# One transformer block: second norm and MLP inside the next batch's attention, one ring for all weight tiles, engine loops written out

## The chip, the cores and the metric

One core of a Trainium2 chip runs the kernel. The metric is the device time of one launch in microseconds. Three runs of the kernel before gave 3036.27, 3036.28 and 3037.81; the median is 3036.28.

## The reference

Four sequences of 512 tokens go through one block: an embedding lookup, attention with grouped heads, and a block-diagonal MLP on permuted features.

```python
h = tok(x)                     # sum of 8 shard lookups with clipped index, + 8 * bias + position
h = h + attn(layernorm(h))     # 32 heads in 8 groups of 4, head size 128, causal softmax, one k and v per group
h = h + ffn(layernorm(h))

def ffn(x, up, down, perm):    # 16 blocks of 64 features, 256 hidden each
    t = x.reshape(b * l, Dm)[:, perm].reshape(b * l, h, d)
    t = gelu(einsum('bhd,hdm->bhm', t, up), approximate=False)
    t = einsum('bhm,hmd->bhd', t, down)
    return t.reshape(b * l, h * d)[:, unperm].reshape(b, l, Dm)
```

Everything is float32, with 4 batches, 512 tokens and 1024 features.

## The kernel before

Every float32 factor is split into a rounded high part (float32r, a copy on ScalarE) and a low part (the rest: a subtraction on VectorE, or on GpSimd for weights), and each product is three matmuls (L403 to L405: high by high, low by high, high by low). Activations are held with features on the partitions, 8 blocks of 128 x 512.

The work is a list of named steps, and every engine walks the same list in order, doing its own part of each step. Nothing is reordered at run time: an engine that waits in one step holds up its part of all later ones. The steps:

- `S0`..`S3`: scores of a head of the group (L424), row maxima (VectorE, L827), exponentials (ScalarE, L655). `N0`..`N3`: scaling of its rows by the inverse sum (VectorE, four operations, L837).
- `Ta`, `Tb`: transposes of the probabilities (L436), rounded by ScalarE (L661 to L667), low part by VectorE (L842 to L851). `PV`: probabilities by values (L457), rounded at L670, low part at L855.
- `Q0`..`Q3`, `K`, `V`: projections, 24 matmuls each (L476). Q0, Q1, K and V of a unit belong to the next group; Q2 and Q3 to the present one. `VT` transposes V.
- `D0`..`D7`: a tile of the dense layer of the group before, 12 matmuls (L487), added to the residual `hacc` by VectorE (L871).
- `H`: the residual is transposed in from the gathered token rows (L517). `G`, `A`, `B`, `La`, `Lb`, `X`: gather of the token rows by GpSimd, addition of positions (GpSimd, L1043) and of the shard edges (a small product, L534, added by VectorE), layer norm per token, and transposes into the normalised input `xn`.

A unit is one group of one batch. A batch is `FIRST`, six turns of `MID` in a loop, `LAST`, and `POST`; the four batches are a loop of three and a copy (L321 to L323). `POST` has the last group's dense tiles, the sums for the second norm (`M`, `R`: matmuls by a matrix of ones, L567), the projections for the next batch, and then `I` and `F`: the MLP, alone, in 8 pairs of blocks (L573). Of a pair, four products `up` (3 matmuls each) go into the two banks of `fb`, ScalarE applies gelu (L754), VectorE rounds (a cast, L963) and takes the low part (L966; of the first of four, GpSimd, L1074), and four products `down` add up in one bank. The input of a pair is gathered from a scratch copy in DRAM (GpSimd, L1051), centred and scaled by VectorE, rounded by ScalarE, low part by VectorE (L946). The output rows are scattered by GpSimd (L1065).

Jobs (projections, dense tiles, `up` products, `H`) alternate between the two banks of `fb`; a job waits for the semaphore of the bank that the job two before it used (L470). Edge products use `sc`, the input transposes `tp`, the MLP outputs `pv` and `sc`.

Weights come by SP's DMA queue into raw buffers: two of 128 x 1024 for the projections with three slots of high and low parts (`RQ`), two of 128 x 512 for the dense layer with four slots (`RD`), and two slots each for the MLP's. ScalarE rounds a tile in the step of the job that frees its slot, GpSimd takes the low part (L996, L1001), and SP loads the next tile once GpSimd is done with a raw buffer. The last of MID's order is `S3 PV1 K N3 Q1 Ta3 PV2 Tb3 V PV3 VT`.

Of the kernel before, what the change touches and what calls it, by code (L numbers as in the profile page):

```python
# [39 lines left out]


# [14 lines left out]
POST = ("D0 X0 X1 M0 D1 X2 X3 M1 D2 X4 X5 M2 D3 X6 X7 M3 D4 M4 D5 M5 D6 M6 D7 M7 Q0 R0 R1 K R2 R3 Q1 R4 R5 R6 R7 "
        "I V VT F").split()
POST_PE = ("D0 X0 X1 D1 M0 X2 X3 D2 M1 X4 X5 D3 M2 X6 X7 D4 M3 D5 M4 D6 M5 D7 M6 Q0 M7 K R0 R1 Q1 R2 R3 R4 R5 R6 R7 "
           "V VT F").split()
START = "G A0 B0 B1 A1 B2 B3 A2 B4 B5 A3 B6 B7 La Lb X0 X1 X2 X3 X4 X5 X6 X7 Q0 K Q1 V VT".split()


def is_job(s):

    return s[0] in "QKDH" or s == "V"  # L80


def number(steps, which):

    out, n = {}, 0
    for s in steps:
        if which(s):
            out[s] = n
            n += 1
# [3 lines left out]
def is_qkv(s):

    return s[0] in "QK" or s == "V"


def is_split_job(s):

    return s[0] in "QK"  # L100


class Place:

    def __init__(self, steps, b, g, kind):
        self.b, self.g, self.steps, self.kind = b, g, steps, kind
        self.n = 8 * b + g
        if kind == "start":  # L110
            self.half, self.split, self.wq = 0, 0, 0
        elif kind == "post":
            self.half, self.split, self.wq = 56 + 76 * b, 3 + 40 * b + 37, 4 + 48 * b + 44
        else:
            self.half, self.split, self.wq = 2 + 76 * b + 7 * g, 3 + 40 * b + 5 * g, 4 + 48 * b + 6 * g
        self.wd = 64 * b + 56 if kind == "post" else 64 * b + 8 * (g - 1)

        self.wq_tile = 0 if kind in ("start", "post") else 4 + 6 * g
        self.wd_tile = 56 if kind == "post" else 8 * (g - 1)
        self.jobs = number(steps, is_job)  # L120
        self.splits = number(steps, is_split_job)
        self.weights = number(steps, is_qkv)

    def bank(self, s):
        return self.jobs[s] % 2

    def full(self, s):

        return 2 * self.half + (self.jobs[s] + 1)

    def free(self, s):

        return self.half + self.jobs[s] // 2

    def split_done(self, s):
        return self.split + (self.splits[s] + 1)

    def wq_at(self, s):

        return self.wq + self.weights[s]  # L140

    def wq_slot(self, s, n, ahead=0):
        first = {"start": 0, "post": 48}.get(self.kind, 4)
        return (first + self.weights[s] + ahead) % n
# [1004 lines left out]
```

## Time and profile before

| what | us |
|---|---|
| median of three runs | 3036.28 |
| span of the profiled execution | 3036.1 |
| first scores, from the start | 92.3 |
| one unit of MID | 75.75 |
| MLP of a batch, alone | 80.6 |
| busy: TensorE, VectorE, ScalarE, GpSimd | 2774.6, 1627.7, 1243.6, 1047.4 |

PE is TensorE, PEld its weight loads, DVE VectorE, ACT ScalarE, POOL GpSimd, SP SyncE. PEclk is the granted share of TensorE's clock: 1.00 is 2.4 GHz, 0.50 is 1.2 GHz. Matmuls are pipelined, so the duration of one is longer than its pace; the pace is read from start to start.

### The profile page before, as it was taken

The page shows a single profiled execution, that of the slowest core. Times are in us where ns is not written, and L with a number is a line of the kernel's source. Part 1 is how long each engine was busy: PE and PEld are TensorE (multiplying, and loading weights), DVE is VectorE, ACT ScalarE, POOL GpSimd, SP SyncE. Part 2 cuts the span into 40 slices and gives each one's busy share as a digit, 9 for nine tenths or more (in the row PEclk, how much of TensorE's full clock was granted, in tenths as well). Part 3 has the DMA queues.
Part 4 walks back from the last instruction along what each step waited for, and adds up shares of the span by engine and source line. Part 5 has one row for each costly group of instructions (what it writes and reads, how often), then busy time and mean ns, then how long its engine had stood idle before and what let it go on. Part 6 is the DMA issues. An engine that isn't in the chain of part 4 may idle for free.

```text
span 3036.1 us, 42337 instructions
## 1 busy us (share of the span) xinstructions
PE 2774.6 (91%) x13344; PEld 2291.2 (75%) x13344; DVE 1627.7 (54%) x3524; ACT 1243.6 (41%) x2791; POOL 1047.4 (34%) x647
## 2 busy tenths in 40 slices
PE   2899999988789999998879999999877999999966
PEld 1788888876578888886657888888756888888844
DVE  4444444455844444446675444444586444444558
ACT  2434444435344444444434444444344444444343
POOL 3433333323443333332435333333153333333224
PEclk9999999999899999999989999999988999999978
DMA  3322222213232222221323222222232222222121
GB/s 103 102 93 69 69 69 69 69 46 108 91 112 70 69 69 69 69 69 46 104 74 118 70 69 69 69 69 69 64 96 77 70 69 69 69 69 69 45 87 63
DMA packets 88977, 229.31 MB, mean 76 GB/s; under 512 B 10781, under 2 KB 10781, under 8 KB 88778
## 3 DMA queue, kind: packets, MB, share of 16 engines
q1 hardware_dynamic: 81450, 202.87, 21.0%
q0 software_dynamic: 7424, 25.17, 2.5%
q8 instruction: 52, 0.85, 0.1%
q14 instruction: 51, 0.42, 0.0%
HBM read 211.22 MB, written 16.78 MB: 75 GB/s over the span
## 4 chain that ended last, share of the span: by engine, by line
PE 81%; DVE 9%; issue 5%; ACT 4%; POOL 1%; DMA 1%; DVEq 0%; SPq 0%; ACTq 0%; POOLq 0%
PE fb L403 19%; PE fb L404 19%; PE fb L405 19%; PE tp L436 4%; DVE g_hi L963 3%; PE sc L403 3%; PE pv L403 3%; PE sc L404 3%; PE sc L405 3%; PE pv L404 3%; PE pv L405 3%; PE sc L567 1%; DVE h_tok L887 1%; DVE y_lo L946 1%; ACT row_buf L638 0%
## 5 line engine op out<-in xcount | busy, mean ns | idle before, releaser
L996 POOL TENSOR_TENSOR wq_lo<-wq_raw,wq_hi 128x1024 fp32r<-128x1024 f32 x193 | 462.6, 2397 | 1238.2 <-ACT wq_hi L617 1234.0
L403 PE MATMUL fb<-xn_hi,wq_hi 128*128 128x512 f32 x1536 | 609.3, 397 | 13.5 <-ACT hacc L695 12.1
L404 PE MATMUL fb<-xn_lo,wq_hi 128*128 128x512 f32 x1536 | 604.6, 394 | 0.0
L405 PE MATMUL fb<-xn_hi,wq_lo 128*128 128x512 f32 x1536 | 604.0, 393 | 0.0
L1001 POOL TENSOR_TENSOR wd_lo<-wd_raw,wd_hi 128x512 fp32r<-128x512 f32 x256 | 331.6, 1296 | 511.4 <-ACT wd_hi L627 494.0
L403 PE MATMUL fb<-at_hi,wd_hi 128*128 128x512 f32 x1024 | 411.9, 402 | 6.2 <-DVE at_lo L855 6.2
L655 ACT ACTIVATE prob<-sc,neg_max 128x128 f32<-128x128 f32 (+3 forms) x512 | 263.3, 526 | 370.7 <-DVE neg_max L830 370.7
L404 PE MATMUL fb<-at_lo,wd_hi 128*128 128x512 f32 x1024 | 404.7, 395 | 0.0
L405 PE MATMUL fb<-at_hi,wd_lo 128*128 128x512 f32 x1024 | 404.5, 395 | 0.0
L403 PEld LDWEIGHTS fb<-xn_hi,wq_hi 128*128 128x128 f32 x1536 | 292.6, 190 | 75.3 <-ACT hacc L695 9.7
L871 DVE TENSOR_TENSOR hacc<-hacc,fb 128x512 f32<-128x512 f32 x256 | 175.7, 686 | 313.5 <-PE fb L405 312.6
L405 PEld LDWEIGHTS fb<-xn_hi,wq_lo 128*128 128x128 f32 x1536 | 291.7, 190 | 61.8
L404 PEld LDWEIGHTS fb<-xn_lo,wq_hi 128*128 128x128 f32 x1536 | 292.2, 190 | 60.1
L627 ACT ACTIVATE wd_hi<-wd_raw 128x512 fp32r<-128x512 f32 x240 | 152.0, 633 | 370.4 <-PE fb L405 351.4
L855 DVE TENSOR_TENSOR at_lo<-pv,at_hi 128x512 fp32r<-128x512 f32 x128 | 88.6, 692 | 348.9 <-ACT at_hi L670 348.3
L837 DVE TENSOR_SCALAR prob<-prob,inv_sum 128x128 f32<-128x128 f32 (+3 forms) x512 | 258.1, 566 | 4.5
L827 DVE CUSTOM_DVE_ANT_0 sc<-sc,mask 128x128 f32<-128x128 f32 (+3 forms) x512 | 236.3, 521 | 15.5 <-PE sc L405 14.8
L677 ACT ACTIVATE q_hi<-fb 128x512 fp32r<-128x512 f32 x128 | 76.6, 599 | 399.8 <-PE fb L405 399.8
L403 PEld LDWEIGHTS fb<-at_hi,wd_hi 128*128 128x128 f32 x1024 | 192.4, 188 | 50.3 <-issue 5.3
L405 PEld LDWEIGHTS fb<-at_hi,wd_lo 128*128 128x128 f32 x1024 | 192.3, 188 | 46.6
L404 PEld LDWEIGHTS fb<-at_lo,wd_hi 128*128 128x128 f32 x1024 | 192.6, 188 | 42.8
L859 DVE TENSOR_TENSOR q_lo<-fb,q_hi 128x512 fp32r<-128x512 f32 x128 | 88.5, 691 | 242.6 <-ACT q_hi L677 242.6
(140 smaller groups left out, 4796.3 us busy)
## 6 DMA issues: line engine op xcount, KB each, us to landing
wq_raw<-in_w_qkv SPq DMA_DIRECT2D x193, 512.0 KB, 3.5
wd_raw<-in_w_dense SPq DMA_DIRECT2D x256, 256.0 KB, 2.6
row_buf<-in_pos SPq DMA_DIRECT2D x16, 512.0 KB, 3.4
h_rows<-hacc SPq DMA_DIRECT2D x32, 256.0 KB, 2.0
up_raw<-in_w_up SPq DMA_DIRECT2D x32, 256.0 KB, 2.6
dn_raw<-in_w_down SPq DMA_DIRECT2D x32, 256.0 KB, 2.8
hacc<-in_x_row SPq DMA_DIRECT2D x3, 256.0 KB, 3.8
hacc<-h_rows,perm POOLq DMA_INDIRECT x32, 3.8
```

Of the source, the lines that this page charges most:

```text
L403: pe.matmul(dst, a_hi, b_hi, start=first, stop=False)
L404: pe.matmul(dst, a_hi, b_lo, start=False, stop=False)
L405: return pe.matmul(dst, a_lo, b_hi, start=False, stop=last)
L436: return pe.transpose(tp[:, bank, c:c + P], prob[:, P_OFF[t] + j * P:P_OFF[t] + (j + 1) * P], ident[:, :])
L627: act.activation(wd_hi[:, m % RD, :], wd_raw[:, m % 2, :], copy).then_inc(wd_rounded, 1)
L655: act.activation(prob[:, P_OFF[t]:P_OFF[t] + w], sc[:, bank, c:c + w], ACT.Exp, bias=neg_max[:, t:t + 1], scale=SCALE, accum_out=row_sum[: ...
L827: dve.tensor_tensor_reduce(at, at, mask[:, S - w:S], 1.0, LOWEST, ALU.add, ALU.max, row_max[:, t:t + 1]).then_inc(tile_max, 1)
L837: dve.tensor_scalar(at, at, inv_sum[:, t:t + 1], None, ALU.mult).then_inc(prob_ready, 1)
L871: dve.tensor_tensor(hacc[:, i, :], hacc[:, i, :], fb[:, place.bank(s), :], ALU.add)\
L963: dve.tensor_copy(g_hi[:, w // 2, w % 2, :], gelu_out(w)).then_inc(g_rounded, 1)
L996: pool.tensor_tensor(wq_lo[:, slot, :], wq_raw[:, raw, :], wq_hi[:, slot, :], ALU.subtract)\
L1001: pool.tensor_tensor(wd_lo[:, m % RD, :], wd_raw[:, m % 2, :], wd_hi[:, m % RD, :], ALU.subtract)\
```

## The change

The loops are gone: the program makes one list of all steps of all batches, and every engine's code is written out from it. The second norm and the MLP of batch b run in units 0 to 5 of batch b+1; only those of the last batch stay behind the last unit (`REST` and what follows it). New step letters: `Z` (transposes of the residual, statistics per token by VectorE), `Y` (mean and inverse deviation spread over the partitions by a product with ones, now float32), `F` (gather of a pair's input), `P` (that input centred by GpSimd, scaled by VectorE, rounded by ScalarE, low part by VectorE), `U` (an `up` product with gelu and, now, the rounding copy on ScalarE; low parts of even ones on GpSimd, of odd ones on VectorE), `O` (a pair's `down` products, 12 matmuls, added by VectorE to the gathered input, and scattered). In the lists small letters `f p u o` are the unit's first pair and `F P U` its second, whose `O` is the next unit's `q`. `Z`, `Y`, `B`, `X`, `U` and `O` are jobs in the two banks of `fb` like the others.

All weight tiles are 128 x 512, in one ring: 4 raw slots (`RAW`), 11 slots of high and low parts (`RW`). A projection takes two tiles. Tile m is rounded in the step of the user of tile m - 11, never before the step of an earlier tile; a pair's `up` tile has its last `U` as user. The positions are loaded straight into the token buffer, and the gather adds the rows to them (no `A` steps). Semaphores are per buffer.

```diff
+RAW, RW = 4, 11
-MID = ("S0 N0 Q2 D0 Ta0 D1 Tb0 S1 N1 Q3 D2 Ta1 D3 Tb1 S2 D4 D5 N2 D6 D7 PV0 "
-       "Ta2 Q0 Tb2 S3 PV1 K N3 Q1 Ta3 PV2 Tb3 V PV3 VT").split()
...
+FIRST = ("S0 N0 Q2 H0 H1 Ta0 H2 Tb0 S1 N1 Q3 H3 Ta1 H4 H5 Tb1 S2 H6 H7 N2 PV0 Q0 Ta2 Tb2 S3 PV1 K N3 Q1 Ta3 "
+         "PV2 Tb3 V PV3 VT")
+MID = ("S0 N0 Q2 D0 Ta0 D1 Tb0 S1 N1 Q3 D2 Ta1 D3 Tb1 S2 D4 D5 N2 D6 D7 PV0 Ta2 Q0 Tb2 S3 PV1 K N3 Q1 Ta3 "
+       "PV2 Tb3 V PV3 VT")
+STATS = ("S0 N0 Q2 D0 Ta0 D1 Tb0 S1 N1 Q3 D2 Ta1 D3 Tb1 S2 D4 D5 N2 D6 D7 Z0 PV0 Z1 Ta2 Z2 Q0 Z3 Tb2 S3 Z4 PV1 K "
+         "Z5 N3 Ta3 Q1 Z6 PV2 V Z7 Tb3 PV3 VT")
+MLP0 = ("S0 N0 Q2 Y0 H0 Ta0 Y1 H1 Tb0 f S1 H2 N1 Q3 H3 D0 p Ta1 H4 D1 Tb1 H5 S2 F D2 H6 N2 D3 H7 D4 D5 D6 D7 u0 PV0 u1 "
+        "Ta2 u2 Q0 u3 Tb2 S3 P PV1 o K N3 U0 Ta3 Q1 U1 PV2 V U2 Tb3 U3 PV3 VT")
+MLP = ("S0 N0 Q2 q D0 Ta0 f D1 Tb0 S1 N1 Q3 p D2 Ta1 D3 Tb1 S2 F D4 D5 N2 D6 D7 u0 PV0 u1 "
+       "Ta2 u2 Q0 u3 Tb2 S3 P PV1 o K N3 U0 Ta3 Q1 U1 PV2 V U2 Tb3 U3 PV3 VT")
+GATHER = ("S0 N0 Q2 q D0 G Ta0 D1 Tb0 S1 N1 Q3 D2 Ta1 D3 Tb1 S2 D4 D5 N2 D6 D7 PV0 Ta2 Q0 Tb2 S3 PV1 K N3 Q1 Ta3 "
+          "PV2 Tb3 V PV3 VT")
+EMBED = ("S0 N0 Q2 D0 B0 Ta0 D1 B1 Tb0 S1 N1 Q3 D2 B2 Ta1 D3 B3 Tb1 S2 D4 D5 N2 D6 D7 B4 PV0 B5 Ta2 Q0 B6 Tb2 S3 B7 "
+         "PV1 K N3 Q1 Ta3 PV2 Tb3 V PV3 VT")
+TURN = ("S0 N0 Q2 D0 Ta0 La D1 Tb0 S1 N1 Lb Q3 X0 Ta1 D2 X1 Tb1 S2 D3 D4 N2 X2 D5 X3 D6 X4 D7 X5 PV0 X6 Ta2 X7 Tb2 S3 "
+        "PV1 Q0 N3 K Ta3 Q1 PV2 Tb3 V PV3 VT")
+LAST = ("S0 N0 Q2 D0 Ta0 D1 Tb0 S1 N1 Q3 D2 Ta1 D3 Tb1 S2 D4 D5 N2 D6 D7 PV0 Ta2 Tb2 S3 PV1 N3 Ta3 PV2 Tb3 PV3")
+REST = "D0 D1 D2 D3 Z0 D4 Z1 D5 Z2 D6 Z3 D7 Z4 Z5 Z6 Z7 Y0 Y1"
...
+def schedule():
+    steps = unit(START, -1, 7)
+    for b in range(B):
+        steps += unit(STATS if b else FIRST, b, 0)
+        for g in range(1, 5):
+            steps += unit((MLP0 if g == 1 else MLP) if b else MID, b, g)
+        if b + 1 < B:
+            steps += unit(GATHER, b, 5) + unit(EMBED, b, 6) + unit(TURN, b, 7)
         else:
+            steps += [s for s in unit(GATHER, b, 5) if s.kind != "G"] + unit(MID, b, 6) + unit(LAST, b, 7)
+    steps += unit(REST, B, 0)
...
+        for m in range(RW, len(self.tiles)):
+            place = max(place, self.at[user[m - RW]])
+            self.splits[STEPS[place]].append(m)
...
+            def start_job(s):
+                if before(s) > 0:
+                    pe.wait_ge(bank_free[bank(s)], before(s))
+                return fb[:, bank(s), :]
...
+                elif s.kind == "P":
+                    n = PAIRS * s.b + s.i
+                    act.wait_ge(scaled, n + 1)
+                    if n > 0:
+                        act.wait_ge(job_full, full(Step("U", (n - 1) // PAIRS, 0, 4 * ((n - 1) % PAIRS) + 3)))
+                    act.activation(y_hi[:, :], y_raw[:, :], copy).then_inc(y_rounded, 1)
+                elif s.kind == "U":
+                    p, w = s.i // 4, s.i % 4
+                    n = 2 * (PAIRS * s.b + p)
+                    act.wait_ge(job_full, full(s))
+
+                    if n > 0 or w > 1:
+                        act.wait_ge(g_low_dve if w % 2 else g_low_pool, n + w // 2)
+                    act.activation(g_raw[:, w % 2, :], fb[:, bank(s), :], ACT.Gelu).then_inc(bank_free[bank(s)], 1)
+                    if p > 0 and w == 0:
+                        act.wait_ge(job_full, full(Step("O", s.b, 0, p - 1)))
+                    act.wait_ge(*free(s))
+                    act.activation(g_hi[:, w, :], g_raw[:, w % 2, :], copy).then_inc(g_rounded, 1)
+                for m in splits[s]:
+                    act.wait_ge(job_full, full(tally.user[m - RW]))
+                    split(m)
...
+                for m in splits[s]:
+                    if m + RAW < NT:
+                        sp.wait_ge(w_ready, m + 1)
+                        load(m + RAW)
```

On GpSimd, `low(m)` for the same tiles stands at the end of each step, behind the step's own gather, scatter, centring or low part. VectorE's part of a `Z` is one statistics operation; at `Z7` four aggregations, a reciprocal and eight scalings of the identity follow, with a square root on ScalarE between.

## Rows read from the trace of the kernel before

**Rows 1.** By stage: length; busy PE, PEld, DVE, ACT, POOL; PEclk, DMA share, GB/s.
```profile
0.00:92.29 92.29, 37.50 (x140) 27.16 (x141) 34.27 (x52) 21.08 (x26) 30.30 (x20) 1.00 0.31 100
...
236.64:312.39 75.75, 75.71 (x383) 64.06 (x382) 36.01 (x91) 30.88 (x75) 24.65 (x15) 1.00 0.22 69
...
752.40:832.96 80.56, 55.91 (x196) 40.15 (x194) 71.74 (x87) 33.00 (x58) 40.77 (x31) 0.87 0.26 83
2895.38:2948.34 52.96, 36.75 (x128) 24.75 (x129) 30.44 (x38) 21.35 (x34) 17.25 (x14) 0.78 0.38 114
2948.34:3036.10 87.76, 56.28 (x192) 41.85 (x192) 72.02 (x85) 30.21 (x54) 38.88 (x30) 0.81 0.19 60
```

**Rows 2.** Order of time, TensorE: start us, us, engine, line, operation; then idle before.
```profile
99.80 0.60 PE L523 MATMUL fb<-ident,h_tok 128*128 128x128 f32 x4
100.24 1.04 PE L436 MATMUL tp<-ident,prob 128*128 128x128 f32 x8
...
904.05 0.39 PE L403 MATMUL fb<-xn_hi,wq_hi 128*128 128x512 f32 x1
...
909.52 0.40 PE L403 MATMUL fb<-at_hi,wd_hi 128*128 128x512 f32 x1
...
912.32 1.03 PE L436 MATMUL tp<-ident,prob 128*128 128x128 f32 x8
```

**Rows 3.** Order of time, TensorE, two products of the MLP at full clock.
```profile
3002.13 0.39 PE L403 MATMUL fb<-y_hi,up_hi 128*128 128x512 f32 x1
...
3002.82 0.39 PE L403 MATMUL sc<-g_hi,dn_hi 128*128 128x512 f32 x1
```

**Rows 4.** Order of time, all engines, from K's end to head 3's turn in a plain unit.
```profile
295.88 0.39 PE L403 MATMUL fb<-xn_hi,wq_hi 128*128 128x512 f32 x1
...
296.08 0.60 ACT L677 ACTIVATE k_hi<-fb 128x512 fp32r<-128x512 f32 x1 [2.59 <-PE fb L405]
...
296.71 0.69 DVE L859 TENSOR_TENSOR k_lo<-fb,k_hi 128x512 fp32r<-128x512 f32 x1 [2.50 <-ACT k_hi L677]
...
297.52 3.45 DVE L837 TENSOR_SCALAR prob<-prob,inv_sum 128x128 f32<-128x128 f32 x4
...
297.71 2.39 POOL L996 TENSOR_TENSOR wq_lo<-wq_raw,wq_hi 128x1024 fp32r<-128x1024 f32 x1 [7.17 <-ACT wq_hi L617]
...
301.33 0.71 PE L436 MATMUL tp<-ident,prob 128*128 128x128 f32 x5
```

**Rows 5.** Order of time, VectorE: the four scalings with GpSimd idle.
```profile
840.26 1.28 DVE L837 TENSOR_SCALAR prob<-prob,inv_sum 128x128 f32<-128x128 f32 x4
```

**Rows 6.** Groups of instructions: busy us, mean ns of one, idle before.
```profile
L627 ACT ACTIVATE wd_hi<-wd_raw 128x512 fp32r<-128x512 f32 x240 | 152.0, 633 | 370.4 <-PE fb L405 351.4 <-DMA wd_raw<-in_w_dense 19.0
...
L1001 POOL TENSOR_TENSOR wd_lo<-wd_raw,wd_hi 128x512 fp32r<-128x512 f32 x256 | 331.6, 1296 | 511.4 <-ACT wd_hi L627 494.0 <-ACT wd_hi L673 17.1
```

**Rows 7.** Order of time: maxima, exponentials and what follows them, one head.
```profile
288.71 0.30 DVE L827 CUSTOM_DVE_ANT_0 sc<-sc,mask 128x128 f32<-128x128 f32 x1
...
290.85 0.37 ACT L655 ACTIVATE prob<-sc,neg_max 128x128 f32<-128x128 f32 x1 [2.53 <-DVE neg_max L830]
...
292.88 0.61 ACT L670 ACTIVATE at_hi<-pv 128x512 fp32r<-128x512 f32 x1
```

**Rows 8.** Busy time of the projection after a stop of 3.00 us.
```profile
120.73:129.00 8.27, 8.27 (x24) 6.56 (x25) 0.98 (x3) 0.96 (x2) 1.28 (x1) 0.65 0.36 129
```

**Rows 9.** Order of time in the last MLP: a VectorE cast beside two GpSimd operations.
```profile
3000.48 3.18 DVE L963 CAST g_hi<-g_raw 128x512 fp32r<-128x512 f32 x1 [0.56 <-ACT g_raw L754]
...
3000.82 1.30 POOL L1074 TENSOR_TENSOR g_lo<-g_raw,g_hi 128x512 fp32r<-128x512 f32 x1
...
3002.07 1.29 POOL L1006 TENSOR_TENSOR up_lo<-up_raw,up_hi 128x512 fp32r<-128x512 f32 x1
```

**Rows 10.** DMA issues of the page: size, median us from issue to landing.
```profile
wd_raw<-in_w_dense SPq DMA_DIRECT2D x256, 256.0 KB, 2.6
```

**Rows 11.** Order of time at the start: the last of four position additions.
```profile
44.25 2.34 POOL L1043 TENSOR_TENSOR h_tok<-h_tok,row_buf 128x1024 f32<-128x1024 f32 x1 [3.52 <-DMA row_buf<-in_pos]
```

More of the change, by code:

```diff
@@ L71 @@
[L71 to L89, printed above, removed]
-    return out
@@ L93, in is_qkv @@
[L93 to L113, printed above, removed]
-        else:
[L115 to L144, printed above, removed]
@@ new lines, with __init__ @@
+STEPS = schedule()
+JOBS = ("Q", "K", "V", "D", "H", "Z", "Y", "B", "X", "U", "O")
+class Tally:
+    def __init__(self):
+        jobs = [s for s in STEPS if s.kind in JOBS]
+        self.at = {s: n for n, s in enumerate(STEPS)}
+        self.job = {s: n for n, s in enumerate(jobs)}
+        self.qk = {s: n for n, s in enumerate(s for s in jobs if s.kind in ("Q", "K"))}
+        self.tiles, self.tile, user = [], {}, []
+        for s in jobs:
+            if s.kind in ("Q", "K", "V"):
+                which = {"Q": s.i, "K": HQ, "V": HQ + 1}[s.kind]
+                own = [("qkv", 2 * ((HQ + 2) * s.g + which) + half) for half in range(2)]
+            elif s.kind == "D":
+                own = [("dense", 8 * s.g + s.i)]
+            elif s.kind == "U" and s.i % 4 == 0:
+                own = [("up", s.i // 4)]
+            elif s.kind == "U":
+                self.tile[s] = self.tile[Step("U", s.b, 0, s.i - s.i % 4)]
+                user[self.tile[s]] = s
+                own = []
+            elif s.kind == "O":
+                own = [("down", s.i)]
+            else:
+                own = []
+            if own:
+                self.tile[s] = len(self.tiles)
+            self.tiles += own
+            user += [s] * len(own)
+        self.user, self.splits, place = user, {s: [] for s in STEPS}, 0
+        for m in range(RW, len(self.tiles)):
+            place = max(place, self.at[user[m - RW]])
+            self.splits[STEPS[place]].append(m)
@@ L147, in tower_kernel, with bank, full, before @@
 def tower_kernel(nc, x_cols, x_row, table, bias, pos, edge_cols, w_qkv, w_dense, w_up, w_down, perm_cols, out):
     scratch = nc.dram_tensor("h1_rows", [E, S], F32).ap()
+    weights = {"qkv": w_qkv, "dense": w_dense, "up": w_up, "down": w_down}
+    tally = Tally()
+    job, splits, tiles = tally.job, tally.splits, tally.tiles
+    NT = len(tiles)
+    def bank(s):
+        return job[s] % 2
+    def full(s):
+        return job[s] + 1
+    def before(s):
+        return job[s] // 2
+    def head(s):
+        return 4 * (8 * s.b + s.g) + s.i
```

1184 lines of the change are left out of this document (496 added, 688 removed).

## The prediction

> **What bounds the kernel now.** I read the busy times by stage first, then TensorE's order of time for the pace of each step, then one head's chain over all engines. An attention unit in the middle takes 75.75 us and TensorE works in 75.71 of them; VectorE is busy 36, ScalarE 31, GpSimd 25 [rows 1]. That unit is pure TensorE work at the full clock. The MLP is not: 80.56 us with TensorE busy 55.91 at a mean clock of 0.87, VectorE busy 71.74 [rows 1]. Start and end are latency too: 92.29 us before the first scores, and 52.96 + 87.76 us from the last unit's dense products on [rows 1]. So time can be won in three places: start, tail, and what the MLP and second norm take beyond their TensorE work. The other engines have room in the sum; the question is whether each engine's fixed order leaves room at each step, for all engines walk one list of steps.
>
> **Prices.** Start to start at full clock [rows 2]: projection 909.52 - 904.05 = 5.47 us, dense tile 912.32 - 909.52 = 2.80, four transposes 100.24 - 99.80 = 0.44. An MLP product of three matmuls is 3002.82 - 3002.13 = 0.69 [rows 3]; a pair needs four up (2.75) and four down (2.75), 5.5 us, eight pairs 43.8.
>
> **The work** if TensorE never waited, from the first scores to the last unit's end. Eight units are 606.0 us a batch. Batch 0: less 8 dense tiles (22.4), plus token and input transposes (8 x 0.44 each, 7.0) and eight edge products (1.9): 592.5. Batches 1 and 2: 606 + 7.0 + 1.9, plus 8 statistics transposes 3.5, two row broadcasts (1.0, as four transposes each; four times that at most), 43.8 of MLP: 663.2 each. Batch 3: less four projections (21.9), plus 3.5 + 3.5 + 1.0 + 43.8: 635.9. Sum 2554.8.
>
> **Waits that the new lists make.** I follow each engine through the MLP unit. The plain unit leaves little slack: K's product ends at 295.88, ScalarE rounds it at 296.08 for 0.60, VectorE takes the low part at 296.71, then come the four scalings of head 3, 3.45 us from 297.52 to 300.97, and TensorE turns that head at 301.33, because Q1's 5.47 us stand between [rows 4].
> (a) Head 3's turn. The MLP lists say K N3 U0 Ta3 Q1: only 0.69 us of TensorE work stands between K and the turn, while the scalings end 5.09 after K. TensorE waits 4.4. Undisturbed, the scalings take 1.28 [rows 5] and the wait is 2.2; that is the low end. I take 4.4, since GpSimd's two low parts after K (2 x 1.30 [rows 6], in place of the single one of 2.39 [rows 4]) start before the scalings. The statistics list (K Z5 N3 Ta3) has the same: Z5 covers 0.44, wait 4.7.
> (b) The input pair. "Q3 p D2 Ta1 D3 Tb1": GpSimd must first do Q3's two low parts, so centring ends about 5.3 after Q3 (0.7 + 2 x 0.63 of ScalarE, overlapped by GpSimd, then three operations of 1.30 [rows 6]). Scaling 0.69, rounding 0.63, low part 0.69 follow; VectorE and ScalarE stand in P meanwhile, then D2 and the turn's own split (0.6 + 0.7) come. Tb1 can run 8.8 after Q3; TensorE has D2, Ta1, D3 = 6.4. Wait 2.4 (1 to 4).
> (c) PV3 stands after Tb3 with U3 between, not V. ScalarE has v_feat, U2's gelu and copy, and Tb3's copy behind V, some 2.5 us with 0.4 of VectorE, PV3 is asked for at 1.6: wait 1.4 (0.5 to 2.8). In the statistics list, Z7's moments, two diagonals and a root on ScalarE stand there: wait 4.3 (3 to 6).
> (d) The ring. A tile is rounded at the step of the user eleven tiles back, in order. An up tile counts as used at its last product, so U0's tile and the four of Q1 and V are all split at U3: five on ScalarE, with four raw slots. The fifth must wait for GpSimd's first low part (1.30) and a load of 2.6 [rows 10]; ScalarE stands until about 9.0 after V. Behind it are PV3's and VT's roundings, so VectorE reaches the next S0 at 11.0, not at 7.6. Maxima take 2.1 and exponentials 2.0 [rows 7], scalings 1.3, Q2's low part 0.7: 17.5 undisturbed, 20 with GpSimd's lock. With the output product behind Q2, D0 shares Q2's bank and is due at 15.6. Wait 3.8 (2 to 6), 12 times.
> (e) The clock. Where TensorE idled 3.00 us before 120.73, the next projection took 8.27 us at a mean granted clock of 0.65, instead of 5.47 [rows 8]: back at the lower level, 1.2 GHz, for part of it. After (a) and (d) I charge 2.0 and 1.6 (0 to 5 together).
> An MLP unit thus waits 3.8 + 2.4 + 4.4 + 1.4 + 3.6 = 15.6. The first of a batch, without the wait of (d) but with H0 behind Q2 (1.5): 12.6. Statistics unit: 0.5 + 4.7 + 4.3 + 3.5 of clock = 13.0. The gather unit has (d): 5.4. Embed and turn units 2.0 together. Per batch 1 and 2: 13.0 + 12.6 + 3 x 15.6 + 5.4 + 2.0 = 79.8. Batch 3: 13.0 + 12.6 + 46.8 + 5.4, and 7.9 for its last unit, which has no projections to cover head 3 (rounding, low parts and scalings of some 2 to 3 us at three places) = 85.7. Batch 0: 3.8 for three turns of its first unit with little between their halves, and 1.5. Sum 250.6.
>
> What decides (a) and (d) is that a single VectorE cast, begun at 3000.48, lasted 3.18 us, more than the four undisturbed scalings together, until two GpSimd operations that began at 3000.82 and 3002.07 had ended, the second at 3003.36 [rows 9].
> The Trainium skill (SBUF — State Buffer, "Who interferes with whom") says otherwise on the order: whichever operation issues first holds the shared ports for its whole instruction and the other blocks. By that rule the scalings would slip in between GpSimd's two low parts and end 1.1 us sooner; over 15 such places the sum would be 16 us lower. The row shows the later GpSimd operations winning, so the sum goes by the row.
>
> **Start.** Four position blocks cost 3.52 of waiting for the load and 2.34 of GpSimd each [rows 11]; they vanish, as the gather adds onto the loaded positions. VectorE's part (four operations of 0.69 a block) becomes the bound, 12.5 us instead of 23.4, but gathers now wait for all four position loads, so it begins later. I take 6.5 less (11 less to 3 more): first scores at 85.8. The eleven first weight tiles cost GpSimd 14.3 behind the gathers and are just covered; uncovered, some 5 us.
> **Tail.** Eight dense tiles 22.4, transposes 3.5, statistics lagging 2, moments and root 5, broadcasts 1.7, gather 5 (it waits for the second broadcast), first input 3.4: 43 against 52.96. The lone MLP has the same chain per pair: two products, the output product, two products, then P; ScalarE now makes gelu and copy (1.2 each): 88 against 87.76. Together 131.5.
> Moved steps that cost nothing: table loads (two to gelu and two back per MLP unit, run in ScalarE's idle time), two gathers and two scatters per unit on GpSimd (taken at 1.3 each like a low part, 5 of the 50 us in which it is idle), and the position loads on SP; if GpSimd's wait for those outlasts the four raw slots, 0 to 3 us a batch. Written-out code has no loop end, but is fetched once and straight on.
>
> **Sum.** 85.8 + 2554.8 + 250.6 + 131.5 = 3022.7, plus 0.2 outside the span: 3023. The profiled span is 3036.1 and the median 3036.28, so they are one number. That is 0.4% less; a measurement can tell about 0.2%, 6 us, from no change. What is hidden, 3 x (80.56 - 43.8) = 110 us of MLP beyond its products and what the norm between batches idled, is nearly given back in many small waits.
>
> **Rivals.**
> 1. The waits form only in part. With (a) at 2.2, (b) at 1.0, (c) at 0.5, (d) at 1.0 and no clock lost, an MLP unit waits 4.7 and all waits sum to some 100: 2872. For: the plain unit runs without a wait on a slack of 0.36 us, and busy times leave room everywhere. Against: (a) follows from the order alone, and (d) from five tiles for four slots. Chance 0.25.
> 2. Slower: ScalarE's stand at U3 lasts longer, because GpSimd, which holds low parts, gathers and scatters in one order, comes late to the first of the five. Place: the fifth split of each MLP unit. Price 6 us and 2 more of clock, 12 times: +96, 3119; it decides from (3042 - 3023) / 12 = 1.6 us per unit on. For: every low part, gather and scatter stands in one queue, in the order of the list. Against: GpSimd idles half of the unit. Chance 0.22.
> 3. The waits are as sized, but start and tail give nothing back (6.5 + 9.2): 3039, no change. Chance 0.08.
> My forecast is the waits as sized, each sum within a sixth: 2985 to 3060, chance 0.45. Of it 0.27 lies below 3030, 0.05 within 0.2% of before, 0.13 above. So faster 0.25 + 0.27 = 0.52, the same 0.08 + 0.05 = 0.13, slower 0.22 + 0.13 = 0.35.
> Range: 2880 to 3085. The low end takes in most of rival 1 (about 0.1 is left below it), the high end (d) at 6, (b) at 4 and the clock at 5, and the milder half of rival 2 (0.1 above it).
>
> **What would show it.** The first scores near 86; plain units of batch 0 still 75.75; MLP units 100 to 104 with about 12 us of TensorE idle, of which 4.4 before head 3's turn with VectorE's scalings as releaser, about 4 before D0 on Q2's low part, 2.4 before Tb1; ScalarE idle 2 to 3 us at the fifth split on a weight load; GpSimd idle half the unit; after the last PV3, 131. If MLP units come out near 90, (a) to (d) are wrong; above 108, rival 2.

## The result, and the profile after

The changed kernel takes 3093.34 us (median of 4 runs, 3092.01 to 3103.49) against 3036.28 before: a ratio of 1.0197, with a 95% interval of 1.0183 to 1.0210. It is slower by 1.8 to 2.1%. Forecast were 3023, and 3085 as the high end. The profiled execution spans 3090.4 us.

The page of the changed kernel, its busy times and its granted clock:

```profile
PE 2751.3 (89%) x13360; PEld 2293.1 (74%) x13360; DVE 1356.6 (44%) x3303; ACT 1354.8 (44%) x3073; POOL 1113.8 (36%) x886
...
PEclk9999999999999999999999999999999999999976
```

No engine but TensorE is over half busy, and the granted clock is 90% or more in all but the last two of the 40 slices. None of TensorE's waits in this trace is put to the issue of its instructions (26.1 us were before), so nothing here points at the written-out code. The time by stage shows where it lies (columns as in [rows 1]): start, a plain unit, a gather unit of batch 0, a statistics unit, an MLP unit, a gather unit of batch 1, the norm behind the last unit, and the last batch's own MLP.

```profile
0.00:87.17 87.17, 37.53 (x140) 27.21 (x141) 29.69 (x53) 25.06 (x38) 31.09 (x27) 1.00 0.46 123
226.51:301.82 75.31, 75.18 (x383) 64.03 (x382) 35.58 (x91) 31.52 (x81) 25.47 (x21) 1.00 0.24 71
452.44:537.39 84.95, 78.05 (x384) 65.88 (x382) 36.65 (x91) 31.41 (x81) 31.70 (x25) 0.94 0.40 112
697.45:789.48 92.03, 82.65 (x415) 70.47 (x414) 43.84 (x113) 33.56 (x83) 27.03 (x22) 0.95 0.28 86
1090.99:1189.39 98.40, 89.98 (x432) 74.93 (x430) 42.11 (x101) 49.19 (x107) 42.45 (x35) 0.97 0.26 75
1189.39:1279.02 89.63, 80.30 (x395) 67.45 (x393) 37.06 (x92) 34.08 (x85) 37.93 (x30) 0.96 0.44 121
2889.07:2931.61 42.54, 29.12 (x132) 21.87 (x133) 14.33 (x32) 9.12 (x14) 13.49 (x11) 0.95 0.34 111
2931.61:3090.40 158.79, 67.83 (x192) 46.43 (x192) 25.99 (x38) 45.92 (x77) 49.03 (x42) 0.71 0.08 25
```

Set beside the forecast's terms (batches end where the next one's first scores begin; batch 3 at the dense products behind its last unit):

| stretch | forecast | profile |
|---|---|---|
| start | 85.8 | 87.2 |
| batch 0 | 592.5 + 5.3 = 597.8 | 610.3 |
| batch 1 | 663.2 + 79.8 = 743.0 | 741.6 |
| batch 2 | 743.0 | 744.1 |
| batch 3 | 635.9 + 85.7 = 721.6 | 706.0 |
| norm behind the last unit | 43 | 42.5 |
| lone MLP | 88 | 158.8 |

Up to the last norm the sum agrees: its dense products begin at 2889.07, forecast at 2891.2. That it agrees so closely is luck, as batch 0 is 12.5 us over and batch 3 is 15.6 us under. The miss of the whole, 71 us, is in the last row. There TensorE is busy 67.8 us of 158.8; before, 56.28 of 87.76 [rows 1]. So 11.5 us of the 71 are the same 192 matmuls at a lower granted clock (0.71 against 0.81), and 59.5 are time in which TensorE stands. TensorE's waits in that stretch (us in all, times, longest):

```profile
PE fb L378 <- DVE y_lo L782: 71.7, 8, 10.3
PE fb L378 <- ACT g_raw L625: 8.4, 7, 1.2
PE fb L378 <- DVE hp L790: 7.4, 7, 1.1
```

The first of the eight stops, 7.68 us, stands ahead of the stretch's first product, as one of 7.72 did before. The next is 6.6 us, and the other six are 9.1 to 10.3 each: one stop a pair, for the input of the next pair. The order of time of one pair shows what stands behind it:

```profile
3004.54 0.80 PE L378 MATMUL fb<-y_hi,w_hi 128*128 128x512 f32 x1 [9.11 <-DVE y_lo L782]
...
3011.13 0.63 ACT L629 ACTIVATE g_hi<-g_raw 128x512 fp32r<-128x512 f32 x1 [4.30 <-PE fb L380]
...
3013.59 0.68 DVE L790 TENSOR_TENSOR hp<-hp,fb 128x512 f32<-128x512 f32 x1
...
3014.55 1.01 POOL L846 DMA_INDIRECT out_rows<-hp,perm_out  x1 [1.43 <-DVE hp L790]
...
3017.57 0.96 POOL L825 DMA_INDIRECT hp<-h_rows,perm  x1 [2.01 <-DMA out_rows<-hp,perm_out]
3018.55 1.27 POOL L840 TENSOR_TENSOR g_lo<-g_raw,g_hi 128x512 fp32r<-128x512 f32 x1
3021.11 1.26 POOL L836 TENSOR_TENSOR y_raw<-hp,mean 128x512 f32<-128x512 f32 x1 [1.29 <-DMA hp<-h_rows,perm]
...
3024.54 0.80 PE L378 MATMUL fb<-y_hi,w_hi 128*128 128x512 f32 x1 [9.26 <-DVE y_lo L782]
```

Two up products and pair p-1's down products run from 3004.54 to 3011.10. ScalarE may not write U0's copy until then (one set of rounded GELUs, all read by those twelve matmuls). The addition follows, the scatter, its landing, only then the gather of pair p+1 into the slot that the scatter has left, its landing, centring, scaling, rounding, low part: 20.00 us from one pair's first product to the next's. Before, all eight gathers went into the residual's eight blocks ahead of the lone MLP, so that no transfer stood in the loop; the input had two sets, the raw GELUs four buffers instead of two, and down products stood one by one between up products, in banks of their own (`fb`, then `sc`, in [rows 3]).

The Trainium skill (DMA: Bandwidth & Descriptors, "Anatomy of one DMA — SWDGE (gpsimd) path") gives a transfer that GpSimd issues a fixed part of some 2.0 us plus its bytes over 436 GB/s, an estimate of 2.6 us for these 256 KB. The trace has medians of 2.8 us (scatter) and 3.4 us (gather) here, 0.2 and 0.8 more. By that split most of each is a price that a smaller tile would not lower; no run here has another size.

Inside the units the forecast's places are there. Head 3's turn, as in [rows 4], now in an MLP unit:

```profile
1162.15 0.60 ACT L573 ACTIVATE k_hi<-fb 128x512 fp32r<-128x512 f32 x1 [2.98 <-PE fb L380]
...
1163.59 3.11 DVE L688 TENSOR_SCALAR prob<-prob,inv_sum 128x128 f32<-128x128 f32 x4
...
1166.76 1.97 PE L398 MATMUL tp<-ident,prob 128*128 128x128 f32 x8 [3.97 <-DVE prob L688]
```

What was not forecast in its size is the gather unit: 84.95 and 89.6 us. Its order of time, and then SyncE's queue over the same stretch:

```profile
475.01 1.53 POOL L810 DMA_INDIRECT h_tok<-in_table,rows  x1 [9.90 <-DMA h_tok<-in_pos]
...
481.54 5.60 POOL L802 TENSOR_TENSOR w_lo<-w_raw,w_hi 128x512 fp32r<-128x512 f32 x4
...
490.68 0.63 ACT L538 ACTIVATE w_hi<-w_raw 128x512 fp32r<-128x512 f32 x1 [12.21 <-DMA w_raw<-in_w_qkv]
491.22 0.37 ACT L566 ACTIVATE pt_hi<-tp 128x256 fp32r<-128x256 f32 x1
...
494.79 0.77 PE L378 MATMUL fb<-at_hi,w_hi 128*128 128x512 f32 x1 [6.76 <-DVE hacc L721]
```

```profile
465.51 1.96 SPq L363 DMA_DIRECT2D h_tok<-in_pos  x4
483.44 4.05 SPq L333 DMA_DIRECT2D w_raw<-in_w_qkv  x4
```

GpSimd stood for the position loads, then issued four gathers, and returned to low parts at 481.54, 16.4 us after its last one. All four raw slots were full until then, so SyncE could load nothing from 467.5 to 483.44; ScalarE stood 12.21 us in a split, with the copy of head 1's second turn behind it, and TensorE 6.76 us behind that.

### The profile page after: what moved, and what is told of

Its sections match the earlier page's. It is cut to its first block, busy times and chain, and to the rows that moved or that the text cites. A ratio compares the mean times of both kernels' runs of the same rounds, so it can differ in the third digit from the quotient of the medians.

```text
span 3090.4 us, 37127 instructions
## 1 busy us (share of the span) xinstructions
PE 2751.3 (89%) x13360; PEld 2293.1 (74%) x13360; DVE 1356.6 (44%) x3303; ACT 1354.8 (44%) x3073; POOL 1113.8 (36%) x886
## 4 chain that ended last, share of the span: by engine, by line
PE 74%; DVE 8%; ACT 6%; DMA 4%; POOL 4%; issue 3%; SPq 0%; ACTq 0%; POOLq 0%; DVEq 0%
PE fb L378 19%; PE fb L380 18%; PE fb L379 18%; PE tp L398 4%; PE sc L379 2%; PE sc L378 2%; PE sc L380 2%; PE pv L378 2%; PE pv L380 2%; PE pv L379 2%; POOL w_lo L802 2%; DVE prob L688 2%; ACT w_hi L538 2%; ACT prob L554 1%; DMA w_raw<-in_w_dense 1%
## 5 line engine op out<-in xcount | busy, mean ns | idle before, releaser
L802 POOL TENSOR_TENSOR w_lo<-w_raw,w_hi 128x512 fp32r<-128x512 f32 x704 | 901.6, 1308 | 1487.1 <-ACT w_hi L538 1486.3
L538 ACT ACTIVATE w_hi<-w_raw 128x512 fp32r<-128x512 f32 x704 | 417.8, 627 | 482.4 <-PE fb L380 355.6
L378 PE MATMUL fb<-xn_hi,w_hi 128*128 128x512 f32 x1536 | 615.9, 401 | 3.3 <-DVE xn_lo L773 1.4
L379 PE MATMUL fb<-xn_lo,w_hi 128*128 128x512 f32 x1536 | 609.0, 397 | 0.0
L380 PE MATMUL fb<-xn_hi,w_lo 128*128 128x512 f32 x1536 | 608.7, 396 | 0.0
L378 PE MATMUL fb<-at_hi,w_hi 128*128 128x512 f32 x1024 | 410.6, 401 | 52.3 <-DVE hacc L721 29.9
L380 PE MATMUL fb<-at_hi,w_lo 128*128 128x512 f32 x1024 | 403.1, 394 | 0.0
L379 PE MATMUL fb<-at_lo,w_hi 128*128 128x512 f32 x1024 | 402.2, 393 | 0.0
L378 PEld LDWEIGHTS fb<-xn_hi,w_hi 128*128 128x128 f32 x1536 | 296.2, 193 | 65.7 <-DVE xn_lo L773 1.8
L379 PEld LDWEIGHTS fb<-xn_lo,w_hi 128*128 128x128 f32 x1536 | 295.7, 193 | 60.8
```

What stands on the lines that cost most here:

```text
L378: pe.matmul(dst, a_hi, b_hi, start=first, stop=False)
L379: pe.matmul(dst, a_hi, b_lo, start=False, stop=False)
L380: return pe.matmul(dst, a_lo, b_hi, start=False, stop=last)
L538: act.activation(w_hi[:, m % RW, :], w_raw[:, m % RAW, :], copy).then_inc(w_rounded, 1)
L802: pool.tensor_tensor(w_lo[:, m % RW, :], w_raw[:, m % RAW, :], w_hi[:, m % RW, :], ALU.subtract)\
```

## The experiments

Theory A: in the lone MLP the return of a gather slot through the scatter sets the pair's 20 us. Theory B: ScalarE's wait for the single GELU set does. Theory C: the lower granted clock (0.71) does. The waits inside the units were tried one by one beside it. Ratios are to the kernel before, on the same chip (its medians there were 3035.1 to 3037.3); gains are differences of medians to 3093.34. The executions of one version lay 1 to 24 us apart, so a gain is good to some 5 us.

**Slots for the gathers**

```diff
+        def hpb(s):
+            return hacc[:, s.i, :] if s.b == B - 1 else hp[:, s.i % 2, :]
...
-        if 0 < p < PAIRS - 1:
-            steps += one("F", p + 1)
+        if 0 < p < PAIRS - 2:
+            steps += one("F", p + 2)
```

> The last batch's pairs get a slot each for their gathered input (the eight blocks of the residual, free by then) and each gather is issued one pair earlier. Theory A (the return of the slot sets the lone MLP's 20.0 us a pair: product of pair p-1, addition, scatter issued, landed 3.0 us later, only then the gather, 3.5 us more, then 3.4 us of centring to low part): what is left of the chain is 6.5 us of products, 5.5 us of ScalarE and 1.4 us to the low part, 13 to 14 us a pair, so the end comes 38 to 48 us earlier, near 3050. Theory B (ScalarE, which keeps U0's copy until pair p-1's products are done because there is one set of four GELU buffers, sets the pace): 0 to 10 us earlier. Theory C (TensorE's lower granted clock makes the pairs long): no change.

3082.02 us, ratio 1.0147 (1.0122 to 1.0171): 11.3 us less. Far from the 38 to 48 of theory A. Its trace tells why:

```profile
2996.11 0.68 DVE L794 TENSOR_TENSOR hacc<-hacc,fb 128x512 f32<-128x512 f32 x1
...
2997.06 1.01 POOL L853 DMA_INDIRECT out_rows<-hacc,perm_out  x1 [1.43 <-DVE hacc L794]
...
2998.37 0.97 POOL L829 DMA_INDIRECT hacc<-h_rows,perm  x1 [0.30 <-issue]
...
2999.13 3.28 DVE L790 TENSOR_TENSOR g_lo<-g_raw,g_hi 128x512 fp32r<-128x512 f32 x1 [2.35 <-ACT g_hi L633]
2999.37 1.27 POOL L847 TENSOR_TENSOR g_lo<-g_raw,g_hi 128x512 fp32r<-128x512 f32 x1
3000.59 1.26 POOL L843 TENSOR_TENSOR y_raw<-hacc,mean 128x512 f32<-128x512 f32 x1
3002.33 0.68 DVE L784 TENSOR_TENSOR y_raw<-y_raw,rstd 128x512 f32<-128x512 f32 x1
```

The waits of 2.01 and 1.29 us for landings are gone, but GpSimd's list still puts scatter, gather, low part and centring of the next pair in a row behind pair p-1's addition, and VectorE's low part (0.69 alone) now lasts 3.28 beside them. VectorE is busy 44.6 us in the lone MLP where it was 26.0, for the same 38 operations. The slot was one link; GpSimd's order is another over the same span. TensorE's stops for the input fell by 13.9 us, from 71.7:

```profile
PE fb L382 <- DVE y_lo L786: 57.8, 8, 9.1
```

**A second GELU set**

```diff
+        def gs(s):
+            odd = s.b == B - 1 and (s.i // 4 if s.kind == "U" else s.i) % 2
+            return (at_hi, at_lo) if odd else (g_hi, g_lo)
```

> The last batch's odd pairs use a second set of GELU buffers (those of the attention output, free by then), the rest is as after the change. Theory A: the chain of product, addition, scatter, gather stays; only the 2.4 us in which the addition stands behind U1's low part vanish: 7 x 2.4 = 17 us at most, near 3076. Theory B: ScalarE's standing of 4.3 to 4.5 us a pair was the bound: 30 us or more. Theory C: no change.

3075.72 us, ratio 1.0126 (1.0107 to 1.0145): 17.6 us less, as theory A had it for this run, and not B's 30. Its trace shows which stops went: the 8.4 and 7.4 us for `g_raw` and the addition, while the stops for the input are what they were:

```profile
PE fb L382 <- DVE y_lo L787: 71.9, 8, 10.4
```

So neither the slot nor the set alone sets the pair's time. C, which had no change here and in the run before, falls as the whole cause: this run gained at a granted clock of 0.70, no higher than after the change.

**Slots and second input set, with and without the GELU set**

```diff
+        def ys(s):
+            odd = s.b == B - 1 and (s.i // 4 if s.kind == "U" else s.i) % 2
+            return (q_hi[:, 0, :], q_lo[:, 0, :]) if odd else (y_hi[:, :], y_lo[:, :])
...
+        if p + 1 < PAIRS:
+            steps += one("P", p + 1)
         steps += one("U", 4 * p + 2) + one("U", 4 * p + 3)
-        if p + 1 < PAIRS:
-            steps += one("P", p + 1)
```

> Slots and the second input set, but one GELU set. Theory A with the GELU set as second limit: the pair goes round by U0, U1, products of p-1 (6.5 us), then ScalarE's copy, GELUs and copies (5.5 us) before the next two: 12 us or so a pair, 50 to 58 us less than after the change, so 10 to 20 us worse than all three together. If the GELU set costs nothing once the gathers are early, it equals all three.

> Slots, second GELU set and a second set of the rounded input together, the next pair's input prepared before the third product of this one. Theory A: a pair falls to 9 to 11 us, where TensorE's products at the granted clock (24 matmuls) or ScalarE's 5.6 us with its waits bound it: 65 to 75 us less than after the change, near 3023, which is below the kernel before. Theory C: pairs stay above 15 us, less than 35 us gained.

Without the GELU set 3063.02 us (ratio 1.0087, 1.0063 to 1.0110), with it 3042.95 (1.0035, 1.0015 to 1.0055): 30.3 and 50.4 us less. The set is worth 20 us here, at the end of its range and about what it gave alone; both runs fall short of their expectation by 15 to 28 us. The second input set was not tried by itself. What is left with all three, TensorE's waits in the lone MLP:

```profile
PE fb L390 <- DVE q_lo L796: 16.5, 4, 5.0
PE fb L390 <- DVE y_lo L796: 15.0, 3, 5.0
```

**GpSimd's order**

```diff
+        if p + 1 < PAIRS:
+            steps += one("P", p + 1)
         if p > 0:
             steps += one("O", p - 1)
-        if 0 < p < PAIRS - 2:
-            steps += one("F", p + 2)
-        if p + 1 < PAIRS:
-            steps += one("P", p + 1)
         steps += one("U", 4 * p + 2) + one("U", 4 * p + 3)
+        if p < PAIRS - 3:
+            steps += one("F", p + 3)
```

> Tail as in the run with all three (slots, GELU set, input set), with the next pair's centring put before the scatter of the pair before, and the gather behind the fourth product. In that run a pair took 13.4 us and TensorE stood 5.0 us a pair for the input's low part, while GpSimd did scatter (1.0), gather (1.0) and centring (1.27) in this order behind the addition. If GpSimd's order is the remaining limit, the stand goes and a pair takes 8.4 to 10 us: 3.4 to 5 us a pair over seven pairs, 22 to 35 us less than that run, 3008 to 3020. If TensorE's half clock is the limit, the products grow into the room: under 10 us less.

3032.57 us, ratio 0.9983 (0.9971 to 0.9994): 10.4 us less than with all three, 60.8 less than after the change. The stage rows of all three and of this version:

```profile
2932.19:3041.70 109.51, 65.76 (x192) 45.56 (x192) 28.49 (x38) 44.02 (x77) 49.09 (x41) 0.75 0.11 36
```

```profile
2942.48:3037.00 94.52, 61.18 (x192) 42.45 (x192) 29.91 (x38) 44.71 (x77) 50.24 (x41) 0.81 0.13 42
```

By the two profiles the lone MLP is 15 us shorter, by the medians of ten the kernel is 10.4 faster (the profiled execution was this version's slowest, and came to the lone MLP 10 us later). That is under half of the 22 to 35 expected, and close to the rival's under 10. But the rival's reason is not seen: TensorE's products did not grow, they shrank from 65.8 to 61.2 us. The stops for the input are gone but for the first two pairs; a new one took part of their place:

```profile
PE fb L390 <- DVE hacc L804: 18.0, 6, 4.2
```

The addition of pair p-1 now stands on VectorE behind the next pair's scaling and low part, and it holds one of the two banks. With the tail mended and nothing else, the kernel is level with the one before: the tail's 60.8 us are the whole of the loss of 57.

**GpSimd's gathers later in the gather unit**

```diff
-GATHER = ("S0 N0 Q2 q D0 G Ta0 D1 Tb0 S1 N1 Q3 D2 Ta1 D3 Tb1 S2 D4
+GATHER = ("S0 N0 Q2 q D0 G Ta0 D1 Tb0 S1 N1 Q3 D2 Ta1 D3 Tb1 S2 g D4
...
-                if s.kind == "G":
+                if s.kind == "g":
                     pool.wait_ge(rows_ready
```

(on GpSimd; SyncE keeps its loads at G)

> The position loads stay where they are, but GpSimd comes to its wait for them and to the four gathers only after head 2's scores, some 30 us later in the unit. If GpSimd's standing is what stops TensorE (gaps of 6.8, 8.0 and 7.9 us in the three gather units, and the granted clock at half for some 7 to 10 us behind them), the three units fall from 84.9, 89.6 and 89.6 us to 76 to 81: 20 to 30 us in all. Rival: the position loads and gathers (4 MB a batch) take the DMA queues' time and the weight tiles are late for that, wherever GpSimd stands: less than 6 us in all.

3062.66 us, ratio 1.0097 (1.0072 to 1.0123): 30.7 less. The gather units of batches 0 and 1:

```profile
449.92:525.22 75.30, 75.17 (x383) 64.05 (x382) 38.90 (x91) 31.48 (x81) 31.79 (x25) 1.00 0.47 126
1172.14:1251.88 79.74, 78.29 (x396) 66.23 (x394) 39.52 (x92) 34.16 (x85) 38.11 (x30) 1.00 0.49 136
```

The DMA share is higher than before the edit (0.40 and 0.44), and the stops of 6.76 and 7.96 us are gone; D0's 1.3 us in the second is left. The queues' load was no cause, GpSimd's standing was.

**Head 3's turn behind Q1**

```diff
-"Ta2 u2 Q0 u3 Tb2 S3 P PV1 o K N3 U0 Ta3 Q1 U1 PV2 V U2 Tb3 U3 PV3 VT")
+"Ta2 u2 Q0 u3 Tb2 S3 P PV1 o K N3 U0 Q1 Ta3 U1 PV2 V U2 Tb3 U3 PV3 VT")
...
-"Z5 N3 Ta3 Q1 Z6 PV2 V Z7 Tb3 PV3 VT")
+"Z5 N3 Q1 Ta3 Z6 PV2 V Z7 Tb3 PV3 VT")
```

> Head 3's turn is put behind Q1 instead of before it, in the statistics, first MLP and MLP units (15 units); nothing else. If the wait comes from the order alone, as the prediction's (a) has it, the gaps of 3.97 and 4.21 us go, and with them the 3.4 us at the half clock (3.4 us of products at half speed cost 1.7 us, 6.8 us cost 3.4 us) that follow each: 15 x (4.0 + 1.7 to 3.4) = 85 to 111 us less. Rival: the wait moves to PV3, because head 3's split now stands behind Q1's on ScalarE and VectorE and V and two GELUs crowd behind it: under 45 us less.

3016.46 us, ratio 0.9938 (0.9914 to 0.9962): 76.9 less, 5.1 a unit. One step moved in three lists, and the kernel is 0.6% faster than the one before. The same MLP unit, at the full clock:

```profile
1070.24:1162.74 92.50, 87.12 (x431) 72.69 (x430) 41.95 (x101) 48.92 (x107) 42.62 (x35) 1.00 0.27 80
```

5.9 us here; it is short of the 85 to 111 because Q1 now waits 0.73 us for K's low part, as it uses K's bank with one product between, and D0 some tenths more. PV3's stop stays at 1.1 us, so the rival is not what is seen.

**A fifth raw slot**

```diff
-RAW, RW = 4, 11
+RAW, RW = 5, 11
```

> The kernel after the change with five raw slots in the weight ring instead of four. By the prediction's (d) D0 waits because the fifth of five splits at U3 stands for a slot and its load; with a fifth slot it doesn't, so the gaps of 1.2 to 2.3 us before D0 in the twelve MLP, gather and last-but-two units go and the half clock behind some of them: 15 to 30 us less, near 3070. Rival: D0 waits for Q2's low part behind the maxima, exponentials and scalings of head 0, wherever the ring stands: less than 5 us.

3045.22 us, ratio 1.0039 (1.0024 to 1.0054): 48.1 less, more than either reading. A late gather unit and a late MLP unit:

```profile
451.91:528.75 76.84, 75.41 (x383) 63.96 (x382) 40.32 (x91) 31.57 (x81) 31.71 (x25) 1.00 0.45 124
1802.04:1897.60 95.56, 88.46 (x431) 73.89 (x430) 42.55 (x101) 49.16 (x107) 42.27 (x35) 0.98 0.26 78
```

In MLP units the stop before D0 is gone, as (d) had it. The gather units fell by 8.1, 9.9 and 10.1 us: the fifth slot covers GpSimd's standing too, 28 of the 48. The other 20 are within the 15 to 30 that (d) had.

**The three repairs together** (order, gathers, head 3's turn)

> The three repairs together: tail as in the run before, GpSimd's gathers later, head 3's turn behind Q1. They lie in different stretches of time, so they should add: 3093 less about 75, 25 and 95 = 2900, with 2880 to 2930 by the ends of each. If one wait only takes another's place, less.

2921.14 us, ratio 0.9635 (0.9610 to 0.9659): 172.2 less, where the single gains sum to 60.8 + 30.7 + 76.9 = 168.4. They add, to within the spread of the runs.

**Three more moves, then Q1 behind K, then the fifth slot again**

```diff
-"S0 N0 Q2 q D0 Ta0 f D1 Tb0 S1 N1 Q3 p D2 Ta1 D3 Tb1 S2
+"S0 N0 Q2 q D0 Ta0 f D1 Tb0 S1 N1 Q3 D2 Ta1 D3 Tb1 p S2
...
-K N3 U0 Q1 Ta3 U1 PV2 V U2 Tb3 U3 PV3 VT")
+K N3 U0 Q1 Ta3 U1 PV2 Tb3 V U2 U3 PV3 VT")
...
-Z4 PV1 K Z5 N3 Q1 Ta3 Z6 PV2 V Z7 Tb3 PV3 VT")
+Z4 PV1 Z5 K N3 Z6 Q1 Ta3 Z7 PV2 Tb3 V PV3 VT")
```

> The version with the three repairs, and three more moves in the lists: the pair's input (p) behind Tb1 instead of before D2, head 3's second turn before V and PV3 behind U3 with V between, Z7 (moments and root) before PV2 instead of between V and PV3. By the prediction's (b) and (c) the gaps of 2.03 us before Tb1 (15 places), 1.11 before PV3 (12) and 4.9 before PV3 in the statistics units (3) go: 30 + 13 + 15 = 58 us less at most, 2863; if each half moves elsewhere (p's part of VectorE now stands before head 2's maxima, Z7's before head 3's low part), 25 to 30 less, 2893.

2894.48 us, ratio 0.9530 (0.9514 to 0.9545): 26.7 less, the second of the two readings: half moves elsewhere. The stops before Tb1 and PV3 are gone in the MLP units and the statistics unit fell from 87.5 to 80.31, but D0's stop grew from about 1.4 to 2.5, and one of 0.5 came in.

```diff
-K N3 U0 Q1 Ta3 U1 PV2 Tb3 V U2 U3 PV3 VT")
+K N3 Q1 Ta3 U0 U1 PV2 Tb3 V U2 U3 PV3 VT")
```

> As the run before, and Q1 directly behind K with U0 behind head 3's turn (in the statistics units Z6 before K). Q1 then uses the bank that K doesn't, so the 0.73 us before Q1 go (15 places, 11 us), and Q1's tiles stand before the up tile in the ring, so that three splits instead of five meet at U3 and by (d) the gap before D0 (1.3 to 3.0 us, 12 places) goes as well: 20 to 35 us less than the run before. If (d) is not the ring's doing, only the 11.

2850.27 us, ratio 0.9381 (0.9365 to 0.9396): 44.2 less, more than expected, since the half clock behind D0's stop went as well. The nine MLP units are 41 us shorter in all and the three gather units 9.5; the three statistics units are 8 us longer, with a new stop of 2.6 us before K, for the bank of a `Z`. The MLP unit with three splits at U3 in place of five:

```profile
952.72:1040.76 88.04, 87.27 (x432) 72.75 (x430) 43.41 (x102) 48.84 (x107) 43.05 (x35) 1.00 0.30 84
```

> The version before (all repairs and the new order of Q1) with five raw slots instead of four. In the kernel after the change the fifth slot took 48 us off, through D0 and through the gather units; here the gathers come later and three splits instead of five meet at U3. If these removed the same waits, nothing is left for the slot: 0 to 5 us less, out of the first MLP units' gaps of 1.1 and 2.3 us before dense tiles. If four slots still bind somewhere, 10 us or more.

2851.11 us, ratio 0.9386 (0.9371 to 0.9402): no difference. The list has taken what the slot had given.

## Why the prediction was wrong

- **The step that failed** is the tail: "The lone MLP has the same chain per pair ... 88 against 87.76". It measured 158.8, 71 us more, and the forecast missed by 70. The chain per pair is not the same. I counted the order of products and ScalarE's operations, but not the buffers that the operations share: two slots for gathered input instead of eight, and so a scatter and a gather in the loop; two raw GELU buffers instead of four; one input set instead of two; down products twelve matmuls in a row in the up products' banks. The runs show three of these as links: the slots are 11 us alone and the set of rounded GELUs 18 (its size was as before; what was new is that the twelve matmuls free it all at once), both with the input set 50, and with GpSimd's order 61. The gains roughly add. The slots gave far less than the 38 to 48 that their landings seemed to be worth, because GpSimd's row of operations, and it seems the single input set, lay over the same span. The two raw GELU buffers and the shared banks were changed by no run, so their part is argued only.
- **Rival 2** (slower by ScalarE's stand at U3) had the sign but not the place: MLP units came out at 97 to 102.5, not above 108. That something other than the units could end on the slow side by 70 us was in no rival.
- **(a)** Head 3's turn: 4.4 forecast, 3.97 measured (statistics unit 4.7, 4.21), scalings 3.11 against 3.45. With the half clock behind it, undoing it gave 5.1 a unit, after 0.7 for a new stop at Q1; right.
- **(b)** Tb1: 2.4, measured 2.03. **(c)** PV3: 1.4, measured 1.11; in the statistics unit 4.3, measured 4.9. Right; moving the steps removed them, though half of the gain was lost to other stops.
- **(d)** The ring: 3.8 forecast, 1.2 to 2.3 measured, so the size was 1.5 to 2.6 us too high. The cause was right: a fifth slot, or three splits instead of five, removed the stop.
- **(e)** In the shown MLP unit the clock at 0.97 of 98.40 us is an estimated 3.0 us of lost work, 3.6 charged. An MLP unit was priced at 75.75 + 11.0 + 15.6 = 102.4 and took 98.4 in the middle; the excess of (d) is most of that, and batch 3 came in 15.6 below its forecast mostly for the same reason: its three MLP units are 13.5 below 3 x 102.4. Of the waits' sum one term does not come out of its own parts: the first MLP unit is written as 12.6, and 2.4 + 4.4 + 1.4 + 1.5 and 2.0 of clock are 11.7; that is 3 us in all.
- **The plain unit** was 75.31, not 75.75: 0.44 a unit, some 14 us over the 31 units with dense tiles, which I had not counted as a gain. It lies in the eight dense tiles, whose products follow one another at 0.227 us where it was 0.233 [rows 2]; no run shows why.
- **The gather unit**: "if GpSimd's wait for those outlasts the four raw slots, 0 to 3 us a batch". It does outlast them, and the price was 8 to 10 us a batch in three batches (with GpSimd's gathers later, the three units fell by 28.7 together). Batch 0's excess of 12.5 us is mostly this; its first unit is 3.4 over. The mechanism was named, the term was mis-sized: I took the wait for the loads, and not the four gathers behind it (1.5 each with 0.3 between) nor the load that SyncE can only then start.
- **The port lock**: the forecast took from [rows 9] that a later GpSimd operation wins over a waiting one of VectorE. The scalings were held (3.11 us against the 1.28 of [rows 5]), but the first of the four ended when the second low part had just begun (rows in the last section). The wait of 3.97 lies between the forecast's 4.4 and the 3.3 of the other rule, so this place decides for neither.
- **Start**: 85.8 against 87.17, right. Norm behind the last unit: 43 against 42.5, right.

What stays open: the lone MLP of the mended tail is 94.5 us against 87.76 before; the addition's place on VectorE is seen in its trace, but a third bank or another place for it was not tried. What the clock alone costs there could not be tried, as no edit sets it.

## What to carry to other kernels

- When work is folded into another loop, its buffers are cut to what that loop needs. Price the copy of it that still stands alone again, from its buffers: for each, who must release it, and what lies between release and next use. A scatter and a gather in that circle are 6.2 us from issue to landing here. Still, taking them out of it gave back only 11 us over seven rounds, since other links held the same span: follow every link before one of them is priced.
- A wait on an engine that also feeds a ring costs nothing until the ring is empty, then all at once. Compare its length with slots times the pace of their use, and add what must restart behind it. Here GpSimd's 16.4 us away from four slots stopped TensorE for 6.8 to 8.0 us.
- In a hand-written order, try the smallest moves: one step behind another gave 77 us, another 44, and a slot's 48 were had by order alone.
